# Layer 3's output stage runs inside the three-step walk over the edges, and sums stand three tiles to a PSUM bank

## What is computed

```python
h = jnp.maximum(_layernorm(x, axis=-1), 0.0)
x = x + _L3_gnn_ref(h, edge_index, ...)

# _L3_gnn_ref, with H = 2 heads of 64
q, k, v = nodes @ Wq + bq, nodes @ Wk + bk, nodes @ Wv + bv
alpha = einsum('ehd,ehd->eh', q[dst], k[src]) / sqrt(64)
w = softmax of alpha over the edges of one dst
x = segment_sum(v[src] * w[:, :, None], dst) + nodes @ Wskip + bskip
gate = sigmoid(concatenate([nodes, x], -1) @ Wgate)
fuse = tanh(x @ Wfuse)
return gate * fuse + (1.0 - gate) * nodes
```

## Time and profile before

| | us |
|---|---|
| median of 3 runs | 6170.97 (6169.4 to 6175.23) |
| the profiled execution | 6173.63 |
| its span, first to last instruction | 6171.8 |
| busy in the span: PE, DVE, POOL, ACT | 4203.9, 4076.8, 4085.8, 1202.5 |

### The profile page before, as it was taken

The page is one execution under the profiler, slowest core; times in us unless marked ns, Lnnn a source line. Parts: engine busy times, 40 slices in busy tenths (PEclk is TensorE's granted clock), DMA queues, the critical chain, the costliest instruction groups (busy, mean ns, idle before and its releaser), DMA issues. The chain is left out here.

```text
span 6171.8 us, 89101 instructions
## 1 busy us (share of the span) xinstructions
PE 4203.9 (68%) x19010; PEld 3354.7 (54%) x19010; DVE 4076.8 (66%) x11745; ACT 1202.5 (19%) x3395; POOL 4085.8 (66%) x4200
## 2 busy tenths in 40 slices
PE   4688787856666666797778777444444456677767
PEld 3577676745555555444555555333333345666666
DVE  8455555548888888746666666344444458888886
ACT  5122222221111111451111111011111011111113
POOL 2477777757777774106777777577777767777771
PEclk9987777768888886897888888555555558777777
DMA  2444444434444445165455555222222344444443
GB/s 57 127 114 115 116 115 116 115 97 134 138 133 137 133 138 104 40 279 188 152 159 154 156 159 140 61 66 66 65 67 67 62 119 139 132 138 134 137 130 79
DMA packets 437311, 737.10 MB, mean 119 GB/s; under 512 B 101130, under 2 KB 293347, under 8 KB 430340
## 3 DMA queue, kind: packets, MB, share of 16 engines
q0 software_dynamic: 173296, 436.67, 27.3%
q1 hardware_dynamic: 255028, 289.17, 14.3%
q10 hardware_dynamic: 8592, 6.82, 0.5%
HBM read 613.48 MB, written 120.01 MB: 119 GB/s over the span
## 5 line engine op out<-in xcount | busy, mean ns | idle before, releaser
L1387 POOL DMA_INDIRECT xh<-pair_d,src_i x1658 | 1622.6, 979 | 581.2 <-issue 497.7
L2158 POOL DMA_INDIRECT l2e_rows<-msg_d,msg_i x829 | 798.8, 964 | 444.5 <-issue 228.4
L955 POOL DMA_INDIRECT l0e_rows<-node_d,src_i x832 | 791.6, 951 | 303.8 <-issue 226.4
L811 POOL DMA_INDIRECT l2f_rows<-msg_d,msg_i x829 | 784.8, 947 | 290.3 <-issue 238.9
L1110 PE MATMUL l0e_ps<-l0e_rows,l0e_sel 128*128 128x256 f32 x1664 | 753.6, 549 | 243.8 <-DVE early_acc L1175 184.8
L847 PE MATMUL l2f_ps<-l2f_rows,l2f_sel 128*128 128x128 f32 x1664 | 428.0, 424 | 580.1 <-DVE l2f_sel L866 363.1
L847 PEld LDWEIGHTS l2f_ps<-l2f_rows,l2f_sel 128*128 128x128 f32 x1664 | 373.2, 316 | 662.3 <-DVE l2f_sel L866 399.8
L2271 PE MATMUL l2e_ps<-l2e_rows,l2e_sel 128*128 128x256 f32 x1664 | 536.7, 448 | 188.9 <-DMA l2e_rows<-msg_d,msg_i 142.3
L1175 DVE TENSOR_TENSOR early_acc<-early_acc,l0e_ps 128x264 f32 x832 | 356.9, 429 | 435.0 <-PE l0e_ps L1111 211.0
L878 DVE TENSOR_TENSOR xh<-xh,l2f_ps 128x128 f32 x832 | 239.0, 287 | 545.6 <-PE l2f_ps L847 438.3
L2330 DVE TENSOR_TENSOR l_acc<-l_acc,l2e_ps 128x256 f32 x832 | 348.9, 419 | 303.2 <-PE l2e_ps L2271 299.3
(11 more groups left out here) (434 smaller groups left out, 7679.6 us busy)
## 6 DMA issues: line engine op xcount, KB each, us to landing
l0e_rows<-in_edge_attr_dram SPq DMA_DIRECT2D x832, 64.0 KB, 1.9
msg_d<-l2a_msg SPq DMA_DIRECT2D x50, 1024.0 KB
l1te_local<-local_d SPq DMA_DIRECT2D x52, 512.0 KB
l2e_local<-local_d SPq DMA_DIRECT2D x52, 512.0 KB
l3te_local<-local_d SPq DMA_DIRECT2D x52, 512.0 KB
xh<-pair_d,src_i POOLq DMA_INDIRECT x1658, 2.8
msg_d<-l2e_msg SPq DMA_DIRECT2D x50, 512.0 KB, 3.4
l0e_rows<-node_d,src_i POOLq DMA_INDIRECT x832, 2.7
```

Of the source, the lines that this page charges most:

```text
L811: pool.indirect_dma_start(rows[:, t % R, :], None, table, bass.IndirectOffsetOnAxis(index[:, t:t + 1], 0)) \
L955: pool.indirect_dma_start(rows[:, t % R, 0:D], None, table, bass.IndirectOffsetOnAxis(g.src_i[:, t:t + 1], 0)).then_inc(gathered[t % R], 16)
L1387: pool.indirect_dma_start(rows[:, t % R, :], None, g.pair_d, bass.IndirectOffsetOnAxis(g.src_i[:, t:t + 1], 0)).then_inc(gathered[n % RG], 16)
L2158: pool.indirect_dma_start(rows[:, t % R, :], None, table, bass.IndirectOffsetOnAxis(index[:, t:t + 1], 0)).then_inc(gathered[t % R], 16)
```

## The change

- **Outputs.** The stage l3o is gone. The new class `Outputs` does its work for one block k = s-7 in step s of layer 3's walk (`LAG = 7`), with one PSUM bank `o_po` for all of its matmuls. Its parts are `cap` and `invert` (the sum of the weights, at least 0.5, and its inverse), `take_apart`, `weigh` and `finish` on DVE (the last three for block k-1), `share`, `move`, `shift` and `squash` on ACT, `turn`, `mix` and `gate` on PE, `store` and `fetch` on SP. It visits the windows in their rank order, and after these windows 47 and 48 once more (`EACH = 52` blocks), since windows 48 and 49 are written as 47 until then. Blocks 45 to 47 fall in the walk's last three steps; blocks 48 to 51 follow it.
- **The banks.** `TB3 = 512 // aw`, which is 3 in both walks: three tiles to a bank. Layer 1's walk keeps three banks, layer 3's has two (`NB`), since `o_po` takes one. PE's list puts the sums of tiles 12 to 15 together, and those of tiles 0 to 3 behind `hand_back`.
- **Layer 2's end.** `Nodes` gets `join`, an addition on DVE of x and h, and `stash_d` keeps x + h in the place of x. SP's `keep_x` follows `keep_h` and waits for it.

```diff
+    def join(self, dve, k, first=False):
+        v = self.window(mybir.EngineType.DVE, k)
+        dve.wait_ge(self.normed, k + 1)
...
+        self.nc.vector.tensor_tensor(self.both[:, :], self.x_of(v), self.hc[:, :], ALU.add).then_inc(self.joined, 1)
...
+class Outputs:
...
+    def fetch(self, sp, k):
+        v = self.window(mybir.EngineType.SP, k)
+        if k >= 2:
+            sp.wait_ge(self.done, k - 1)
+        sp.dma_start(self.h[:, k % 2, :], self.g.stash_d[:, self.cols(v, NP)]).then_inc(self.landed[k % 2], 16)
+        sp.dma_start(self.both[:, k % 2, :], self.g.stash_d[:, self.cols(v)]).then_inc(self.landed[k % 2], 16)
...
+    def squash(self, act, k):
+        act.wait_ge(self.gated, k + 1)
+        if k >= 1:
+            act.wait_ge(self.weighed, k)
+        self.nc.scalar.activation(self.gates[:, :, :].rearrange("p k f -> p (k f)"), self.po[:, 0:2 * D],
+                                  ACT.Tanh).then_inc(self.acted, 1)
+
+    def turn(self, pe, k):
+        pe.wait_ge(self.landed[k % 2], 32 * (k // 2 + 1))
+        if k >= 1:
+            pe.wait_ge(self.acted, k)
+        self.nc.tensor.transpose(self.po[:, 0:D], self.h[:, k % 2, :], self.g.ident[:, :]).then_inc(self.turned, 1)
+
+    def mix(self, pe, k):
+        pe.wait_ge(self.moved, k + 1)
+        pe.wait_ge(self.evened, k + 1)
+        self.nc.tensor.matmul(self.po[:, 0:D], self.wskip[:, :], self.ht[:, :], start=True, stop=False)
+        self.nc.tensor.matmul(self.po[:, 0:D], self.z[:, :], self.g.ident[:, :], start=False, stop=True).then_inc(self.mixed, 1)
+
+    def gate(self, pe, k):
+        pe.wait_ge(self.biased, k + 1)
+        self.nc.tensor.matmul(self.po[:, 0:2 * D], self.xt[:, :], self.wf[:, :, :].rearrange("p k f -> p (k f)"),
+                              start=True, stop=False)
+        self.nc.tensor.matmul(self.po[:, 0:D], self.ht[:, :], self.wg[:, :], start=False, stop=True).then_inc(self.gated, 1)
...
+    def cap(self, dve, k):
+        v = self.window(mybir.EngineType.DVE, k)
+        if k >= 1:
+            dve.wait_ge(self.evened, k)
+        self.nc.vector.tensor_scalar(self.den[:, :], self.acc[:, self.part(v, D, self.H)], 0.5, None,
+                                     ALU.max).then_inc(self.capped, 1)
...
         def slot(t):
-            return ps[t // 2 % 3][:, t % 2 * aw:(t % 2 + 1) * aw]
+            return ps[t // TB3 % NB][:, t % TB3 * aw:(t % TB3 + 1) * aw]
...
+                    if late and s >= LAG + 2:
+                        o.store(sp, s - LAG - 2)
+                        o.fetch(sp, s - LAG)
...
-                    if t >= 6 and t % 2 == 0:
-                        pe.wait_ge(added, t - 4)
+                    if t >= TB3 * NB and t % TB3 == 0:
+                        pe.wait_ge(added, t - TB3 * (NB - 1))
...
+                if late:
+                    o.squash(act, NS + 2 - LAG)
+                    for k in range(NS + 3 - LAG, o.EACH):
+                        o.share(act, k)
+                        o.move(act, k)
+                        o.shift(act, k)
+                        o.squash(act, k)
...
-                    dve.wait_ge(summed, t // 2 * 2 + 2)
+                    dve.wait_ge(summed, min(T, t // TB3 * TB3 + TB3))
...
+                if late:
+                    dve.wait_ge(added, T)
+                    for k in range(NS + 2 - LAG, o.EACH):
+                        if k >= NS + 3 - LAG:
+                            o.cap(dve, k)
+                            o.invert(dve, k)
+                        o.take_apart(dve, k)
+                        o.weigh(dve, k)
+                        o.finish(dve, k)
```

359 lines of the change are left out of this document (175 added, 184 removed).

## The result

The changed kernel took 6144.3 us (median of 20 runs) and the kernel before 6166.4 us (median of 20) in the same comparison: a ratio of 0.9962, with an interval of 0.9949 to 0.9975. That is 22 us faster; 23 were forecast. The time forecast was 6148 us.

A forecast was written before the change was run, and what follows sets the result against it. DVE and POOL were taken to bound layer 3's walk almost equally. The terms -53.0 + 36 - 29 + 20 + 3 + 2 - 2 gave -23 us, from 6170.97 to 6148 us, with a range from 6112 to 6192.

The forecast's parts named there:

- End of the program: After layer 3's walk: 88.1 us of output stage go, 35.1 us of last blocks stay; -53.0 us.
- New DVE work: Layer 3's walk: five more DVE instructions per step, 0.8 us each step over 45 steps; +36 us.
- The gather wait: Layer 3's walk: slower DVE finds gathered rows ready, so most of its 35 us wait goes; -29 us.
- Wait for the turned scores: Layer 3's walk: DVE's first scan waits for PE's transpose, delayed by gate and banks; 0.35 us per step.
- Adds at the bank's third tile: Layer 3's walk: DVE's adds wait for the third tile of a bank; 0.1 us more per step.
- Drain: Steps 52 to 54 of layer 3's walk: 0.8 us of new work each and a little for PE; +3 us.
- Layer 2's gather walk and layer 1's banks: Join delays a store at layer 2's end, +2 us; nine tiles in flight cut layer 1's sum waits, -2 us.
- C: Rival: the gathers' wait in layer 3's walk stays, since gathers land late in pieces; 6177 us, chance 0.17.
- E: Rival: new DVE operations stretch the gathers, POOL needs 21.9 us per step; 6207 us, chance 0.04.
- D: Rival: PE becomes the bound in layer 3's walk, each scan waiting 1.4 us and more; 6195 us, chance 0.15.
- B: Rival: no new wait, fuller PE keeps the higher clock and transposes are in time; 6120 us, chance 0.22.
- The clock: Rule weighed for layer 3's walk: 1.1 us or more of new PE work per step would raise PE's clock; counted in B.

The follow-up runs named there:

- e5_tail: The changed kernel with its last four output blocks in banks and tiles of their own, issued phase by phase; ratio 0.9702 to the kernel before, tail 13.8 us.
- e1_ballast: The kernel before with five more DVE instructions per step from step 7 of layer 3's walk on; ratio 1.0015 to the kernel before.
- a1_again: The changed kernel once more, nothing edited, on another chip; ratio 0.9753 to the kernel before, which took 7549 us there.

## Why the prediction was right, point by point

- **End of the program, -53 forecast, -57.6 measured.** The mechanism was right. A block was put at 7.1 us; the four take 7.07, 6.28, 5.91 and 5.98, 3.2 us less in all than reckoned. The three DVE operations were taken 0.5 us apart and are 0.32 (6109.72, 6110.05, 6110.37). The last DVE operations of block 47 end 2.4 us after the last add instead of 1.5, and from the last DVE operation to the end it is 2.9 us instead of 5.2. In the first block PE waits 3.0 us for its load, which the forecast does not have; that just this block meets the 7.1 is chance. That the chains one after the other make the tail is shown by e5_tail.
- **New DVE work, +36 forecast, +35 measured.** DVE's busy time grew by 34.9 us.
- **The gather wait, -29 forecast, -31.6 measured** (35.0 to 3.4). The two traces of the first chip show it in the amount; e1_ballast, which was to show the cause, met chips without that wait, so the cause is argued and not shown.
- **Wait for the turned scores, +16 forecast, about +2.5 to +5 measured.** This term was mis-sized. What the parts leave for it is +4.0 (20.7 - 34.9 + 31.6 - 13.4). DVE stands idle before the first scan for 2.5 us in all, 1.2 of them put down to PE; from the start of the product ahead to the scan it is 5.2 us more than before over the 45 steps. The forecast let 18% of the transposes run at the lower clock with 1.4 us lost each. The 52 transposes now have a mean of 283 ns instead of the 299 of the earlier trace rows, so by the forecast's own working some 7% instead of 18% ran at the lower clock, an estimate from 272 and 421 ns. In the step shown, the sum of gate, banks and transpose came out as reckoned for the higher clock, with nothing to spare and nothing lost.
- **Adds at the bank's third tile, +4.5 forecast, +13.4 measured.** 6.0 of it is one wait in step 51, through PE's transpose of a block whose load took 14 us instead of 1.8 to land. The same kernel's other profile does not have it, so it is not a cost of the change that would come each time. The prediction had named SP's loads but looked only at the mask row behind them. It did not ask whether the block itself would be there for PE, which stands in order and holds up everything for it. Of the other 7.4, 4.9 stand on tile 14 in the steps of one kind of three and 2.3 on tile 15 in those of another, 0.16 us per step instead of 0.1. The places are those of the bank's third tile, as the prediction had it; no run on this chip has the banks without the output stage's matmuls, so that the banks alone make them is argued.
- **Drain, +3 forecast, +5.9 measured.** Beside the new work the scan waits 1.8 us and cap 1.6 us there.
- **Layer 2's gather walk and layer 1's banks, +2 and -2 forecast, -2.4 and +2.0 measured.** Both are within what two profiles of equal code differ by. But the wait for sums in layer 1's walk did not fall: over the whole walk it is 53.5 us in 228 waits where the earlier trace rows has 42.0 in 188. In the 45 steps DVE's adds stand idle 3.2 us more than before, with the same DVE work (797.6 and 797.3 us). So nine tiles in flight instead of six gained nothing there, and the forecast's -2 had the wrong sign.
- **The rivals.** C (the gather wait stays) is out by 3.4 us, E (gathers stretched) by a mean of 1.00 us against its 1.05, and its 23 us in layer 2's walk did not come. There is some truth in it: a gather beside finish takes 0.08 us more, where E had 0.46 and the forecast nothing, after one pair of rows. That pair was no fair sample: in the same 45 steps of the kernel before, 33 of the 196 gathers beside the fp32 operation of the earlier trace rows (and not beside the bf16 one) take 1.30 us in the mean instead of 0.95. In the changed kernel 161 of 710 gathers take over 0.965 us where 70 did, 16.7 us more in all; only 3 us of that stand beside finish. The Trainium skill (SBUF — State Buffer, Who interferes with whom) lets a DVE operation with two SBUF inputs hold up a GpSimd instruction that reads SBUF and not one that only writes it. The gather reads its row numbers from SBUF (`src_i`), so the page does not clear it, as the forecast took it to; the 43 gathers beside finish, longer by 8%, agree with the page, while most of those beside the operation of the earlier trace rows take the usual 0.95 us, which the page does not explain. It cost nothing, since POOL was no longer the bound. D needed steps of 22.1 us and B steps of 20.7; they are 21.09.
- **The clock.** The walk has 0.74 where it had 0.75, with PE busy for 718 us instead of 649; the same 45 steps of layer 1's walk have 0.68 where they had 0.81, with the same number of matmuls and a length of 928.6 us instead of 925.8. So more work did not bring more clock here, and less clock cost almost nothing while DVE was the bound. The Trainium skill (TensorE: Matmul & The Clock Gate, Part 1) has activity release the array's clock; at the granularity of these stretches no run here shows it.

So the total of -22 agrees with the forecast of -23 partly by chance. In the pair of profiles the output stage and the scan came out better than reckoned by 4.6 and 12 us, the adds and the drain worse by 12, and the parts add up to -31.4. That the medians say -22 is owed to executions that differ by some 10 us, which is half of the gain. What is shown is the mechanism's large terms, 57.6 us off the end against 35 us of new work and 32 us of a wait that went; a hit within 1 us is not.

## What to carry to other kernels

When a stage is hidden in a loop, sum what the engines have left after it; but ask of each moved instruction also whether its own data will be there, since an engine with a list in order makes everything behind it wait: one load that took 14 us to land cost this walk 6 us. A stage that leaves a few serial blocks behind the loop still pays each one's whole latency; running the last ones side by side took 30.5 us to 13.8. And a forecast made on one chip holds for that chip's bound: on a chip where TensorE's results came late, the bank layout and the order of sums, which gained nothing in layer 1's walk on the first, were worth 2%. A gain also belongs to the chip on which both kernels ran: compare there before calling one version better.

## What the runs showed of the hardware

- On three chips the same kernels took 20 to 24% longer than on the first. DVE's work (806.8 and 806.4 us), a gather (996 and 1000 ns) and the output stage (90.5 and 88.1 us) take the same. Of the 1207 us by which the span of a1_again is longer, 1151 lie in the stretches in which GpSimd gathers, and in layer 3's walk they are waits of DVE.
- In e1_ballast PE's results come up to 11 us late while GpSimd issues 16 gathers in a row, and 88 of 90 such waits end 1.0 to 3.3 us after the last; in a1_again it is 44 of 60. SP's issues are slower in the same walk: between the two loads of a block its median is 1.32 us in a1_again and 0.6 to 1.4 in the other runs, instead of 0.52. On the first chip 710 gathers follow each other without a pause of over 1 us, and but for SP's issues and the load of step 51 nothing was seen to come late. What differs between the chips, and what it is in the gathers that holds PE's signals up, stays open: it was not tried to take the gathers away.
- Under such waits the releaser that the profile names is a DMA of a stage long past. That, and two engines going on in the same instant, is how they can be told from a real wait.
